# Graph attention, layer 0: the destination one-hot is laid out tile by tile

## The reference

```
xl, xr = x @ W_l, x @ W_r                        # (12500, 128), 4 heads of 32
h   = xl[src] + xr[dst]                          # one row per edge
e   = einsum('ehc,hc->eh', leaky_relu(h, 0.2), att)
p   = exp(e - segment_max(e, dst)[dst])
out = segment_sum(p / segment_sum(p, dst)[dst] * xl[src], dst) + bias + x
```

## Time and profile before

| | |
|---|---|
| median of 3 runs | 4612.28 us (4607.57 to 4612.98) |
| the profiled execution | 4611.55 us, its span 4609.7 us |
| busy over the span | PE 3464.4, PE weight load 2604.3, DVE 2131.5, ACT 577.0, POOL 3181.3 us |
| edge sweep of layer 0, 131 to 2262 us | PE 2017.8, DVE 1473.2, POOL 1577.6 us busy |
| edge sweep of layer 1, 2470 to 4495 us | PE 1103.7, DVE 354.6, POOL 1485.6 us busy |

### The profile page before, as it was taken

The page is one execution under the profiler, slowest core; times in us unless marked ns, Lnnn a source line. Parts: engine busy times, 40 slices in busy tenths (PEclk is TensorE's granted clock), DMA queues, the critical chain, the costliest instruction groups (busy, mean ns, idle before and its releaser), DMA issues. The chain is left out here.

```text
span 4609.7 us, 71384 instructions
## 1 busy us (share of the span) xinstructions
PE 3464.4 (75%) x18612; PEld 2604.3 (56%) x18613; DVE 2131.5 (46%) x7034; ACT 577.0 (13%) x1586; POOL 3181.3 (69%) x3295
## 2 busy tenths in 40 slices
PE   6899999999999999999786555555555555555559
PEld 4555655655655655555465555555555555555557
DVE  7566676667766766766475111111111111111117
ACT  3111111111111111111054000000000000000005
POOL 3777777777777777777333777777777777777750
PEclk9899999999999999999788777777777777777779
DMA  6643433343343343344255333333333333333323
GB/s 180 171 114 108 114 114 109 114 114 111 113 114 112 111 113 113 110 114 114 76 138 100 103 107 103 108 104 107 105 105 107 103 107 103 108 103 107 103 71 114
DMA packets 460317, 512.32 MB, mean 111 GB/s; under 512 B 179918, under 2 KB 360014, under 8 KB 460278
## 3 DMA queue, kind: packets, MB, share of 16 engines
q1 hardware_dynamic: 277526, 262.17, 19.4%
q0 software_dynamic: 100352, 208.93, 16.5%
q10 hardware_dynamic: 82400, 40.77, 3.1%
HBM read 464.25 MB, written 47.30 MB: 111 GB/s over the span
## 5 line engine op out<-in xcount | busy, mean ns | idle before, releaser
L497 POOL DMA_INDIRECT rows<-xl_table,src_idx x1568 | 1586.4, 1012 | 532.6 <-issue 517.4
L1072 POOL DMA_INDIRECT rows<-x_table,src_idx x1568 | 1480.8, 944 | 504.3 <-issue 477.4
L528 PE MATMUL ph<-node_of,xr_win 128*128 128x512 f32 x784 | 752.9, 1095 | 1.3 <-issue 1.3
L1086 PE MATMUL pA<-edge_of,dst_row 128*128 128x128 f32 x1568 | 327.7, 394 | 472.3 <-DMA rows<-x_table,src_idx 389.0
L1086 PE MATMUL pT<-node_of,dst_row 128*128 128x128 f32 x1568 | 324.1, 391 | 437.1 <-DMA rows<-x_table,src_idx 388.3
L1086 PEld LDWEIGHTS pA<-edge_of,dst_row 128*128 128x128 f32 x1568 | 305.9, 299 | 488.3 <-issue 486.9
L1086 PEld LDWEIGHTS pT<-node_of,dst_row 128*128 128x128 f32 x1568 | 302.4, 296 | 452.9 <-issue 451.3
L565 PE MATMUL pA<-wmsg,edge_of 128*128 128x136 f32 x3168 | 426.1, 288 | 7.1 <-DVE edge_of L782 6.6
L565 PEld LDWEIGHTS pA<-wmsg,edge_of 128*128 128x128 f32 x3168 | 385.8, 192 | 11.4 <-issue 8.0
L554 PE MATMUL pT<-att_heads,relu_h 128*128 128x56 f32 x3136 | 390.9, 278 | 1.3 <-DVE shifted L811 1.3
L640 ACT ACTIVATE relu_h<-ph 128x512 f32<-128x512 f32 x392 | 234.2, 597 | 1185.8 <-PE ph L528 1185.8
(11 more groups left out here) (168 smaller groups left out, 4154.1 us busy)
## 6 DMA issues: line engine op xcount, KB each, us to landing
dst_row<-in_dst SPq DMA_DIRECT2D x196, 513.0 KB
dst_row<-in_edge_attr SPq DMA_DIRECT2D x195, 512.0 KB, 3.6
rows<-xl_table,src_idx POOLq DMA_INDIRECT x1568
rows<-x_table,src_idx POOLq DMA_INDIRECT x1568
sums_table<-win ACTq DMA_DIRECT2D x198, 68.0 KB
rows<-in_x SPq DMA_DIRECT2D x100, 128.0 KB, 2.3
xr_win<-xr_table SPq DMA_DIRECT2D x196, 64.0 KB
sums_table<-win ACTq DMA_DIRECT2D x1, 6868.0 KB
```

The lines of the kernel that those rows point to most:

```text
L497: pool.indirect_dma_start(rows[s][:, t, :], None, xl_table[:, :], bass.IndirectOffsetOnAxis(ap=src_idx[s][:, t:t + 1], axis=0))\
L528: return [pe.matmul(h[:, k:k + 4, :], xr_of[:, :], by_tile[:, k:k + 4, :], start=False, stop=stop) for k in range(0, T, 4)]
L1072: pool.indirect_dma_start(rows[s][:, t, 0:D], None, x1_table[:, :], bass.IndirectOffsetOnAxis(ap=src_idx[s][:, t:t + 1], axis=0))\
L1086: ins = pe.matmul(bank, m[:, t, :], one_hot[:, t, :], start=(k == 0 and t == 0), stop=(k == 1 and t == T - 1))
```

## The change

`node_of` is now written in the order of the tiles, (t p), with the edge 8p + t at column 128t + p. DVE's instruction still reads `dst_row` in its order, p outside and t inside, and so writes each result 128 elements, 512 bytes, behind the last. PE's product reads four tiles, 512 columns, one after the other; before, it read them with a step of eight elements, 32 bytes. The same holds for `node_more`. Nothing else changes: the same instructions, sizes and waits.

```diff
+        def in_tiles(t):
+
+            return t.rearrange("n (t p) -> n p t", t=T)
+
...
                     def product(xr_of, one_hot, stop):
-                        by_tile = one_hot.rearrange("n (p t) -> n t p", t=T)
+                        by_tile = one_hot.rearrange("n (t p) -> n t p", t=T)
...
                 def node_one_hot(g):
-                    first, ids = first_node[:, s:s + 1], dst_row[s][:, 1:1 + G]
+                    first, ids = first_node[:, s:s + 1], dst_row[s][:, 1:1 + G].rearrange("n (p t) -> n p t", t=T)
...
-                    v.tensor_scalar(node_of[g.c % 2][:, :], ids, first, None, ALU.is_equal)\
+                    v.tensor_scalar(in_tiles(node_of[g.c % 2][:, :]), ids, first, None, ALU.is_equal)\
                      .then_inc(S("node_of_made"), 1)
...
                 def further_one_hots(g, span):
-                    first, ids = first_node[:, s:s + 1], dst_row[s][:, 1:1 + G]
+                    first, ids = first_node[:, s:s + 1], dst_row[s][:, 1:1 + G].rearrange("n (p t) -> n p t", t=T)
...
-                        v.tensor_scalar(node_more, ids, first, None, ALU.is_equal).then_inc(S("node_more_made"), 1)
+                        v.tensor_scalar(in_tiles(node_more), ids, first, None, ALU.is_equal).then_inc(S("node_more_made"), 1)
```

## The result

| | before | after |
|---|---|---|
| median of 4 runs, same job | 4611.39 us (4607.57 to 4612.98) | 4668.11 us (4666.45 to 4671.1) |
| ratio, 95% interval | | 1.0128 (1.0115 to 1.014) |
| profiled execution, span | 4611.55, 4609.7 us | 4668.35, 4666.5 us |
| POOL's period in layer 0's sweep | 10.77 us | 11.09 us |

The kernel became 57 us slower; forecast were 47 us, 4659 us in all. The four added lines shift all later ones: L497 of before is L501 now, L702 is L706, L528 is L532, L756 is L760, L782 is L786.

The account below looks back on a forecast made before the run. POOL was to pace layer 0's sweep once PE shortened: 9.99 us plus 0.12 of pauses plus 0.90 of held gathers, 11.01 us a group against 10.77, +47 us on 4611.6, giving 4659 us; range 4560 to 4745.

Parts of the forecast that it names:

- POOL becomes the pacer: Layer 0's edge sweep: PE's chain falls to 9.2 us a group, so POOL's gathers set a period of 11.01 us.
- PE's record: PE's four 512-column records per group in layer 0: 0.43 us each instead of 0.93, saving 2.0 us of PE's work.
- the costly rival: The strided one-hot takes 1.95 us and holds POOL throughout: 4812 us, chance 0.08.
- The held time C: Time per group that DVE instructions delay POOL's gathers in layer 0: 0.48 by L756 plus 0.42 by L702, 0.90 us.
- Pauses: POOL's longer pauses between layer 0 gathers: about 0.12 us a group kept, half of the 0.24 us.
- PE's wait for rows: PE's wait for gathered rows at L523 in layer 0's sweep grows from 13.7 us to 200 us or more.
- The clock rival: PE, waiting before each group's first product, runs more stretches at 1.2 GHz; chain 11.8 us, 4810 us, chance 0.05.
- DVE's order: The one-hot's extra 0.3 us costs nothing in DVE's own sequence, since DVE waits 0.92 us for PE before L746.
- Fewer collisions: Rival: gathers mostly miss the DVE instructions that hold POOL; held time 0.4 us a group, 4561 us, chance 0.32.
- the point of 0.66: Held time in us a group under which the changed kernel would be faster than before.
- PE gains nothing: Rival: PE's records stay at 0.93 us and PE sets the period; 4612 us, chance 0.05.
- the whole gain: Rival: all 392 us saved on PE become time, 4220 us; given no chance.

Follow-up runs that it names:

- read_weigh_edge: Kernel after, with the node one-hot's stride moved to DVE's reading side and one operand each of L760 and L786 read from PSUM: 4578.25 us, ratio 0.9932.
- dve_only: Kernel after, but PE reads with its old stride, so only DVE's strided write remains and the edges' order is wrong: 4670.39 us, ratio 1.013.
- pe_only: Kernel before, but PE reads the one-hot without a stride while DVE writes it as before, so the edges' order is wrong: 4542.51 us, ratio 0.9855.
- read_side: Kernel after, but DVE reads dst_row with a step of eight elements and writes node_of in one run, same result: 4665.25 us, ratio 1.0122.
- after_weigh_psum: Kernel after, with L760's weights read from PSUM, where ACT writes a second copy: 4667.07 us, ratio 1.0126.

## Why the prediction was right, step by step

**POOL becomes the pacer: right, shown.** POOL has no pause over 0.3 us, its lead over PE is used up (6.9 us before, 2.0 after), and PE waits for rows 93.9 us, 83 of them after the start. In read_weigh_edge 88 us less of held gathers are 87 us less of time at the same DVE lengths. dve_only gives the same time with 1095 ns per record, pe_only 126 us less with a one-hot of 0.76 us.

**PE's record: right, at full clock.** There the records start 0.43 us apart, as predicted. But of the 588 intervals within groups only 192 are 0.4 to 0.5 us, and 340 are 0.8 to 0.9 us, at the lower clock: near the 0.92 us that the stride had cost. The idle before L569 names L786 (31.9 us; 0.81 us in the timeline), but 32 us in all, not 0.8 us a group: PE mostly came late enough, after waiting for rows.

**L706: mis-sized.** 1.05 us predicted, 1.334 measured. The slope of L738, 1.76 ns for each step, was carried over to a write of two elements a step; it is (1.334 - 0.153)/512 = 2.31 ns. On the reading side, (1.152 - 0.153)/512 = 1.95 ns. It stayed far from the 1.95 us of the costly rival.

**The held time C: 0.90 predicted, 1.10 measured.** Its two parts erred in opposite ways. By the count above L706 held POOL 133/196 = 0.68 us a group (0.42 predicted), L760 67/196 = 0.34 us (0.48); the rest is L786 and `prepare`'s L742, for which the prediction had nothing. With the measured 1.33 us put into the prediction's own formula for L706 (0.56 within, 0.76 x 0.5/1.25 = 0.30 ahead), C would have been 0.48 + 0.86 = 1.34: evenly spread gathers were too unkind an assumption.

**Pauses: 0.12 predicted, 0 measured.** None of the 0.24 us of longer pauses was POOL's own; half had been kept. The errors, +0.20 for C and -0.12 for the pauses, make 11.09 instead of 11.01 us, that is +16 us; the 6 us behind the last gather took back a third. That the forecast of 4659 lies 9 us from the measured 4668 is thus in part luck: L706's part alone was 0.26 us a group too small, 51 us.

**PE's wait for rows: 200 us or more predicted, 93.9 measured.** This check failed. The prediction let PE be busy in 76% and idle in the rest; it is busy in 1937.8/2189 = 89%. The granted clock fell to 0.83 (0.97 in the earlier trace rows), below the 0.85 that was named as a warning for the case that PE does not wait, and slower records filled the slack: L532 means 845 ns where four in 1.88 us stand at full clock. The clock rival got its mechanism and not its price, because the slack was there to be used.

**DVE's order: not costless at the loop's ends.** The prediction put 0.3 us on DVE behind the cover of 0.92 us. DVE's "issue" before L750 now is 73.2 us in 48 times, before 16.8 us in 11 times, once per turn of the loop over four groups, with at most 1.6 us. read_weigh_edge and dve_only show the same 73.2 us at different times, so this wait does not set the time by itself. In dve_only it weighs more: PE waited for rows 27.7 us, 11.4 of them at the start, which leaves 0.08 us a group against 0.42 in the kernel after. The first scans of its groups lie 12.1, 11.3, 10.5 and 10.4 us apart over a turn of the loop, before 11.1, 11.0, 10.5 and 10.4. So there the chain of PE and DVE is within 0.1 us as long as POOL's period, and dve_only alone can't tell the two apart. How much of the 126 us between pe_only and after (1.0128/0.9855 = 1.0277) is this chain and how much is held gathers was not settled; the periods put 0.61 x 196 = 120 us of it on POOL's own account, but what made the gathers fall so may include DVE's longer chain. Open too is why four kernels with different holders all have a period of 11.09 or 11.10 us. That the order of gathers against DVE's instructions settles itself, since POOL's delays move DVE in turn, fits read_side and after_weigh_psum, but was only argued.

**The rivals.** Fewer collisions (4561) did not come for this change, but for pe_only (C = 0.49, 4542.5) and read_weigh_edge (0.65, 4578) it did, on the near side of the point of 0.66 that the prediction named. With no pause left that point is really 10.77 - 9.99 = 0.78. PE gains nothing and the whole gain both fell: the gain is real and stops at POOL.

## What to carry to other kernels

Before an engine is made faster, take the floor of the next one from start to start in a stage where nothing disturbs it, here 9.99 us for eight gathers against 10.77: that gap, not PE's 95%, bounds what a saving can bring. A DVE instruction that reads two SBUF tensors or runs two elements a step is paid for twice when POOL issues the gathers, so a stride moved from PE to such an instruction can cost more than it saves. Free such holders together, by an operand in PSUM: here one alone only handed its gathers to the next.

## What the runs showed of the hardware

- The one-hot that moves two elements a step seems to keep that with a write stride of 512 bytes: 1.33 us for 1024 elements, against 0.76 us in a row, 1.15 us with a read step of 32 bytes, and 1.92 us for a strided tensor_tensor.
- Against a DVE instruction with two SBUF operands (L756, L760, L782, L786), only a gather that starts within it is held: of those that start 0.1 to 1.0 us into L756 or L760, all end 0.81 to 0.82 us after it. In the kernel after the 107 gathers that start 0.1 to 0.5 us ahead of L760 take 0.94 us, and L760 keeps its length. So the two don't exclude each other for their whole length, as the prediction had it.
- With one of the two operands in PSUM the same instruction holds none: of 174 gathers that start within L761 in after_weigh_psum the longest took 0.954 us.
- The node one-hot also stretches a gather that is already under way: of those that start up to 0.45 us ahead, all end some 0.12 us after it, although they started first, and it keeps its length (in the kernel after 1.34 us with such a gather, 1.33 without). In read_weigh_edge one that started 0.32 us ahead of L710 took 1.58 us. Those that start 0.55 us ahead or more take 0.94 us.

In the kernel after, a gather 0.38 us ahead of L760 takes 0.94 us, one that starts within it 1.18 us, and one 0.32 us ahead of L706 1.79 us:

```profile
1484.25 0.94 POOL L501 DMA_INDIRECT rows<-xl_table,src_idx  x1 [0.30 <-issue]
1484.63 1.23 DVE L760 TENSOR_TENSOR wmsg<-rows,wmsg 128x1024 f32<-128x1024 f32 x1
1485.50 1.18 POOL L501 DMA_INDIRECT rows<-xl_table,src_idx  x1 [0.30 <-issue]
...
1490.73 1.79 POOL L501 DMA_INDIRECT rows<-xl_table,src_idx  x1 [0.30 <-issue]
1491.05 1.34 DVE L706 TENSOR_SCALAR node_of<-dst_row,first_node 128x1024 f32<-128x1024 int32 x1
```

- PE's float32 records of 512 columns, read with a step of 32 bytes, start 0.92 us apart at full clock, and 0.43 us apart without the step; 0.85 us without it at the lower clock.
